# Down products of the gated layer gathered into fewer places of the attention, and the next rows' transposes moved ahead of the last two

## The reference

```
def _layer(x, wqkv, qs, ksc, wo, lg, lb, w1, b1, w2, b2):
    h = shift_token(x)
    q, k, v = jnp.split(h @ wqkv, 3, axis=-1)      # then 8 heads of 64
    q = l2norm(q) * qs
    k = l2norm(k) * ksc
    q, k = rotary_xpos(q, k)
    o = local_attention(q, k, v)
    x = x + o @ wo
    h = layernorm(shift_token(x)) * lg + lb
    a, g = jnp.split(h @ w1 + b1, 2, axis=-1)
    x = x + (a * gelu(g)) @ w2 + b2                # the "down" product
    return x
```

## Time and profile before

| | us |
|---|---|
| median of 3 runs | 775.01 (774.91 to 777.64) |
| profiled execution: its own time | 773.93 |
| profiled execution: span from first to last instruction | 772.1 |
| PE busy | 719.2 (93%) |
| DVE, ACT, POOL busy | 499.8 (65%), 493.7 (64%), 457.2 (59%) |
| step 9, from its first scores to those of step 10 | 39.08 |

### The profile page before, as it was taken

One profiled execution on the slowest core, in us unless ns is written; L12 is line 12 of the kernel. 1 busy time (PEld: TensorE's weight loads), 2 busy tenths in 40 slices (PEclk: granted clock), 3 DMA queues, 4 the chain that ended last, 5 costly groups with the idle time before them and its releaser, 6 DMA issues.

```text
span 772.1 us, 17016 instructions
## 1 busy us (share of the span) xinstructions
PE 719.2 (93%) x4952; PEld 598.0 (77%) x4952; DVE 499.8 (65%) x1426; ACT 493.7 (64%) x1321; POOL 457.2 (59%) x644
## 2 busy tenths in 40 slices
PE   4999899899999999999999889999999999999967
PEld 3888777587878787878787778878787878787846
DVE  1376773785858585858585867767676767676732
ACT  2556633567676767575758686858575757585742
POOL 1467672596747475757575466747474747474722
PEclk9999995899999999999999999999999999999998
DMA  5665460150000000000000001010101010101000
GB/s 146 225 185 150 116 208 8 56 186 16 27 17 27 14 27 14 27 14 27 14 27 14 28 2 55 2 54 0 54 0 54 0 54 0 54 0 42 2 28 14
DMA packets 32790, 38.41 MB, mean 50 GB/s; under 512 B 8476, under 2 KB 22896, under 8 KB 32752
## 3 DMA queue, kind: packets, MB, share of 16 engines
q1 hardware_dynamic: 32752, 37.95, 15.5%
HBM read 29.55 MB, written 8.39 MB: 49 GB/s over the span
## 4 chain that ended last, share of the span: by engine, by line
PE 66%; issue 11%; DVE 9%; ACT 6%; POOL 6%; DMA 1%; ACTq 0%; DVEq 0%; POOLq 0%; SPq 0%
PE ps L447 38%; PE ps L654 4%; PE ps L613 4%; PE ps L640 3%; POOL pr L1484 3%; PE ps L631 2%; PE ps L625 2%; PE ps L547 2%; ACT pr L924 2%; PE ps L658 1%; PE ps L440 1%; DVE hT_lo L1183 1%; DVE arena L1047 1%; DVE sm L1210 1%; DMA arena<-x 1%
## 5 line engine op out<-in xcount | busy, mean ns | idle before, releaser
L1484 POOL TENSOR_SCALAR pr<-pr,rl 128x128 f32<-128x128 f32 (+1 forms) x256 | 107.9, 434 | 91.1 <-DVE rl L1216 91.0
L924 ACT ACTIVATE pr<-sm,mn 128x128 f32<-128x128 f32 (+1 forms) x256 | 113.5, 448 | 9.9 <-DVE mn L1210 9.1
L447 PE MATMUL ps<-hT_hi,w_hi 128*128 128x256 f32 (+1 forms) x352 | 105.1, 299 | 3.5 <-DVE hT_lo L1183 1.4
L1210 DVE CUSTOM_DVE_ANT_0 sm<-ps,wmask 128x128 f32<-128x128 f32 (+1 forms) x256 | 80.2, 355 | 33.7 <-PE ps L631 31.1
L447 PE MATMUL ps<-hT_hi,w_lo 128*128 128x256 f32 (+1 forms) x352 | 99.5, 283 | 0.0
L447 PE MATMUL ps<-hT_lo,w_hi 128*128 128x256 f32 (+1 forms) x352 | 99.2, 282 | 0.0
L884 ACT ACTIVATE sqb<-ps 128x512 f32<-128x512 f32 x64 | 38.0, 596 | 93.2 <-PE ps L447 92.8
L1454 POOL TENSOR_TENSOR rn<-ss,nhalf 128x16 f32<-128x16 f32 x32 | 94.4, 2950 | 2.7
L447 PE MATMUL ps<-wqkv_hi,yT_hi 128*128 128x512 f32 x192 | 79.2, 413 | 4.0 <-DVE wqkv_lo L1095 2.6
L447 PE MATMUL ps<-wqkv_lo,yT_hi 128*128 128x512 f32 x192 | 76.4, 398 | 0.0
L447 PE MATMUL ps<-wqkv_hi,yT_lo 128*128 128x512 f32 x192 | 76.2, 397 | 0.0
(11 more groups left out here) (168 smaller groups left out, 2135.7 us busy)
## 6 DMA issues: line engine op xcount, KB each, us to landing
arena<-x SPq DMA_DIRECT2D x16, 256.0 KB, 2.9
ystream<-arena SPq DMA_DIRECT2D x16, 256.0 KB, 2.0
y_next<-ystream SPq DMA_DIRECT2D x16, 256.0 KB, 2.8
y_res<-ystream SPq DMA_DIRECT2D x16, 256.0 KB, 2.7
arena<-L_ffn_w SPq DMA_DIRECT2D x5, 640.0 KB, 4.7
arena<-ctx SPq DMA_DIRECT2D x8, 256.0 KB, 4.6
arena<-mask_BxSxS_ik SPq DMA_DIRECT2D x8, 256.0 KB, 3.4
xmid<-arena SPq DMA_DIRECT2D x8, 256.0 KB, 2.1
```

The costliest lines, as they stand in the source:

```text
L447: last = mm(out, lhsT(a), rhs(b), start=(start and i == 0), stop=(stop and i == 2))
L924: A(pr[:, h % NS, a:b], sm[:, h % NS, a:b], ACT.Exp, bias=mn[:, h, t:t + 1], scale=-1.0, accum_out=ls[:, h, t:t + 1]).then_inc(e_done, 1)
L1210: V.tensor_tensor_reduce(sm[:, h % NS, a:b], bank(h % SB)[:, a:b], wmask[:, a:b], 1.0, -NEG, ALU.add, ALU.min, mn[:, h, t:t + 1]).then_inc ...
L1484: G.tensor_scalar(pr[:, h % NS, a:b], pr[:, h % NS, a:b], rl[:, h, t:t + 1], 1.0, ALU.mult, ALU.mult).then_inc(pn_done, 1)
```

## The change

The number that `downs` is called with changes at three places, and the calls behind single heads are gone but for one. Before, the twelve products stood in six groups: 0 to 4, 5 and 6, 7, 8, 9, 10 and 11. After, they stand in four: 0 to 5, 6 to 8, 9, 10 and 11. The transposes of the next rows, which stood behind products 10 and 11, now stand straight behind the eighth head's transposes and ahead of these two products. No instruction is added or taken away, and the other engines' queues are unchanged.

```
-                    downs(5)
+                    downs(6)
                     for h in range(HEADS + 1):
                         if h in (0, 1, 3):
                             scores_own((h + 3) // 2)
                             scores_both((h + 3) // 2)
                         if h == 0:
-                            downs(7)
+                            downs(9)
                         if h < HEADS:
                             tr_probs(h)
-                        downs(min(10, 7 + (h + 1) // 2))
+                        if h == 5:
+                            downs(10)
+                        if h == HEADS - 1 and not (isinstance(s, int) and s == STEPS - 1):
+                            pe.wait_ge(ynext_in, 16 * (s + 2))
+                            pe.wait_ge(mn_done, T * HEADS * (s + 1))
+                            transpose_rows(y_next, 0).then_inc(y_tr, 1)
                         if h and h % 2 == 0 and h < HEADS:
                             weighted(h // 2 - 1)
                     downs(T * HC)
-                    if not (isinstance(s, int) and s == STEPS - 1):
-                        pe.wait_ge(ynext_in, 16 * (s + 2))
-                        pe.wait_ge(mn_done, T * HEADS * (s + 1))
-                        transpose_rows(y_next, 0).then_inc(y_tr, 1)
                     weighted(PAIRS - 1)
```

## The result

| | before | after |
|---|---|---|
| median of 11 runs each, us | 774.91 (773.11 to 777.64) | 778.31 (775.63 to 779.80) |
| profiled execution: its own time, span | 773.93, 772.1 | 779.73, 777.8 |
| from the first scores of step 2 to those of step 7, mean of the 5 steps | 38.87 | 39.10 |
| from the first scores of step 9 to those of step 14, the same | 39.08 | 39.33 |

A forecast was written before the change was run, and what follows sets the result against it. It took the attention to be bound by a chain through PE's scores, DVE's minima and ACT, not by PE's busy share. 3.5 and 0.6 gave 4.1 us, on the median's level 779.1, say 779.0; range 775.0 to 781.4.

The forecast's parts named there:

- The chain through PE's scores, DVE's minima and ACT's `exps(2)` sets the attention's length: Attention: whatever PE issues ahead of the scores of heads 2 and 3 is on the path; products behind them fill time.
- `down(5)` at the front: 0.235 x 15 = 3.5: Ahead of the scores of heads 2 and 3: two matmuls delay ACT's chain by 0.235 us in each of 15 steps.
- The upper bound of 0.35: Most that down(5) ahead of the scores of heads 2 and 3 could cost a step; the lower bound was zero.
- the likeliest case: Front of the attention: a delay of the chain there, chance 0.81, with its own range of 777.5 to 781.4 us.
- `down(7)` and `down(8)` ahead of the first transposes: nothing: First head's transposes start 0.33 later, but ACT is in exps(2) until then: no cost; 0.1 a step without that cover.
- Nothing comes back behind heads 1 and 3: Removing down(7) and down(8) there frees 0.35 of PE twice, but PE just waits longer ahead of later transposes: no gain.
- The next rows' transposes: 0.1 in six steps, 0.6 in all: Ahead of down(10) and down(11): add_down up to 0.17 later in steps 9 to 14, taken as 0.1 each.
- PE does not decide: Rival: PE's own length counts and fewer places are cheaper, saving 0.44 a step, 6.6 in all: 768.4; chance 0.09.
- The delay is not swallowed: Rival: the 0.235 vanishes where ACT waits later, 0.25 ahead of head 3's transposes, so nothing happens: 775.0; chance 0.06.
- TensorE's clock does not fall for want of `down(7)` and `down(8)`: Rival: some 4.4 us of attention without these products drop to 1.2 GHz, costing up to 66: 841; chance 0.04.

The follow-up runs named there:

- The gathering alone: Kernel before with down(5) kept behind the scores of heads 2 and 3, products 5 to 8 ahead of the first head's transposes, down(9) behind the sixth head: 776.61, ratio 1.0016.
- with an earlier `exps(2)`: The whole change, but four products instead of six ahead of the scores of heads 2 and 3: 776.71, ratio 1.0016 to the kernel before.
- the front alone: Kernel before with only down(5) moved ahead of the scores of heads 2 and 3: 779.10, ratio 1.0048.

## Why the prediction came out right, point by point

*The chain through PE's scores, DVE's minima and ACT's `exps(2)` sets the attention's length.* Shown from both sides: 0.23 a step for two matmuls in front, 0.585 for five, and -0.18 for three less, where the start of the scores stops being the limit.

*`down(5)` at the front: 0.235 x 15 = 3.5.* Measured 0.23 to 0.24 a step, with the part alone and with the whole. The upper bound of 0.35, what `down(5)` took behind the scores, was the wrong end: the change from scores to products is paid by whichever product follows the scores, and is not moved along with `down(5)`. In the trace after, `down(6)` pays it: its first matmul takes 0.39 where those in the series take 0.28, and the next starts 0.23 later (496.85 and 497.08), not 0.12. (The other end of the likeliest case's range, 0.17 a step, has no row behind it, and its upper end adds up to 781.3, not 781.4.)

*`down(7)` and `down(8)` ahead of the first transposes: nothing, with `exps(2)` as cover.* Shown. The gathering alone is worth +0.006 and +0.026 a step. The transposes end at 498.24 + 0.27 = 498.51 in the trace after, 0.32 before ACT takes them at 498.83. With the front left as it was some 0.1 remains, and with an earlier `exps(2)` the cover is gone and ACT waits 0.17. So nothing is the right price in this kernel only because the same change makes `exps(2)` late. One link was left out of the argument: the second head's transposes stand behind the scores of heads 4 and 5, and `probs_T(1)` wants them. With the change `exps(2)` is late enough to cover that as well; with an earlier `exps(2)` it cost the last 0.04 of the gain.

*Nothing comes back behind heads 1 and 3.* Shown: from the first weighting on, the distances are those of before to within 0.03. Where `down(7)` stood PE now waits for POOL ahead of head 2's transposes (0.24 at 500.08). Ahead of head 4's, where `down(8)` stood and a wait was expected too, there is none; it comes right behind them, for ACT, ahead of the second weighting (0.22 at 503.49).

*The next rows' transposes: 0.1 in six steps, 0.6 in all.* This is the term that was mis-sized: it is 0. It rested on a delay of `add_down` of up to 0.17, from a last product that comes 0.52 later and a hand-over of 0.51 like the one after the last `wo` product. The product came 0.44 later, the hand-over took 0.43 or less, and DVE is in `low_oT(2)` until then anyway. The trace after has the same: 508.43, then 508.86 with no idle time. Without this term the sum on the median's level would have been 778.5; 778.3 was measured. That the times agree so closely is in part luck: the medians of four experiments lie 0.8 to 1.9 us away from what their steps give.

*The rivals.* PE does not decide: the gathering without the front fills PE's wait, as that rival wanted it, and the steps gain nothing. The delay is not swallowed: 0.24 arrives at the next step's first scores. TensorE's clock does not fall for want of `down(7)` and `down(8)`: the window from 498.00 to 504.40 holds only scores, transposes and weightings, and its granted clock is 1.00 (2.4 GHz). The one fall in steps 1 to 14 of this run lies in step 8, behind a wait of 2.4 us, and comes at about the same place with the front alone, which leaves those products where they were (last section). The Trainium skill (TensorE: Matmul & The Clock Gate, Part 4: PE-mode transpose) says that transposes don't count as busy for the clock as other products do; whether they do can't be told here, since scores and weightings lie between them, but the fall that one could fear from it did not come in this window.

## What to carry to other kernels

When one in-order queue feeds a chain that runs through other engines, filler work cost its full length here where it stood ahead of the instruction that the chain waits for, and next to nothing behind it as long as the chain's next instruction in that queue still came in time, whatever the queue's mean busy share said; the number to read is the idle time of the next engine just ahead of that link. Fewer places for the filler were no gain in themselves, and each gathered piece needs a look at what it pushes back and at what covers that. After a move out of the front has brought something, look for the next limit in the same link: here, by the trace, it was another engine's order, and the cover of a second edit was used up by the gain.

## What the runs showed of the hardware that was not expected

TensorE's clock fell for some microseconds at different places in different runs, and once not after the same wait that it followed in another. Windows of the kernel after, step 8 (columns as above; the clock is the last but two):

```profile
463.00:466.50 3.50, 1.20 (x11) 0.80 (x11) 1.81 (x4) 3.50 (x11) 2.08 (x5) 1.00 0.00 0
466.60:469.90 3.30, 3.30 (x18) 2.88 (x18) 2.94 (x3) 1.66 (x4) 0.69 (x1) 0.50 0.00 0
```

And of the kernel before, step 7, some 20 us behind its first scores, and then the same place of step 8 as above:

```profile
425.00:428.60 3.60, 1.04 (x8) 0.82 (x7) 2.37 (x3) 2.76 (x3) 0.00 (x0) 1.00 0.24 56
428.70:432.00 3.30, 3.30 (x13) 2.82 (x12) 2.86 (x3) 1.64 (x3) 0.00 (x0) 0.50 0.22 85
461.50:463.90 2.40, 0.03 (x1) 0.00 (x0) 1.52 (x3) 2.40 (x11) 0.84 (x3) 1.00 0.00 0
464.00:467.50 3.50, 3.50 (x31) 2.55 (x31) 2.68 (x3) 2.90 (x5) 1.93 (x3) 1.00 0.00 0
```

In step 8 PE stands still for 2.4 us in both kernels (ACT and DVE have other work there), yet of the two only the run after shows the clock down at 0.50 (1.2 GHz) behind it, while PE was fully busy. Before, it stayed at 1.00 there and was down in step 7 instead, also after PE had stood mostly still (1.04 of 3.60 us). It is not the change that decides: of the nine kernels profiled here, five have the fall in step 8, among them the front alone and the next rows' transposes alone, and step 8 took 42.0 to 42.4 us in them; four have not (40.3 to 41.3). Step 0 and the end have such stretches as well (step 0 takes 42.9 to 45.1 us, the stretch from step 15's first scores to the end 47.6 to 49.4); there the clock was down for longer after (second row) than before (first row):

```profile
749.50:756.30 6.80, 4.30 (x19) 3.90 (x20) 0.69 (x1) 3.34 (x7) 0.00 (x0) 0.50 0.00 0
753.30:763.40 10.10, 6.87 (x31) 6.47 (x32) 1.18 (x2) 4.35 (x9) 0.12 (x1) 0.50 0.00 0
```

Single runs of one kernel lie 5 to 6 us apart (772.28 to 777.38 and 772.69 to 778.39 for the kernel before), and most of that goes with the clock: of the 17 runs, the four with a mean granted clock of 0.966 took 776.84 to 778.39, the four with 0.974 or more 772.69 to 773.96. The lengths of steps 3 to 6 and 9 to 13, which are alike to 0.05 within a run, told the parts of this change apart where the medians could not. What decides between a fall and none after the same wait stays open.
